# D*u added on TensorE: a diag(D) matmul under the transposes that bring the scan's output back

## What is computed

```python
xz = jnp.einsum('ble,de->bld', xn, W_in)
u, z = (xz[..., :DIN], xz[..., DIN:])
u = jax.nn.silu(conv(u))                     
dt, Bm, Cm = ...                              # from u
dA = jnp.exp(dt[..., None] * A)               # 16 states for each channel
dBu = dt[..., None] * Bm[:, :, None, :] * u[..., None]
h = dA * h + dBu ;  y = (h * C).sum(states)   # the scan over the 512 tokens
y = y + u * D
y = y * jax.nn.silu(z)
out = jnp.einsum('bld,ed->ble', y, W_out)
```

## Time and profile before

| | us |
|---|---|
| median of 3 runs | 1903.42 |
| lowest and highest run | 1899.98, 1903.66 |
| the profiled execution's time | 1908.13 |
| its span, first to last instruction | 1906.3 |

### The profile page before, as it was taken

How to read it: one execution, slowest core, us unless ns; L and a number is a source line. 1 busy time by engine, 2 the same in 40 slices (tenths; PEclk the granted TensorE clock), 3 DMA queues, 4 the chain that set the end, 5 groups by cost and what they waited for, 6 DMA issues and landing times. The chain is left out here.

```text
span 1906.3 us, 15651 instructions
## 1 busy us (share of the span) xinstructions
PE 1431.9 (75%) x5136; PEld 789.3 (41%) x5136; DVE 1516.7 (80%) x1606; ACT 937.5 (49%) x1481; POOL 793.6 (42%) x411
## 2 busy tenths in 40 slices
PE   5556676776788679976788679886788769876965
PEld 2345233343345235453355335453355334452433
DVE  3987699967898799969998699968999699963242
ACT  4432654435653655636553645626563555633522
POOL 0665165514554155523554156523555055530000
PEclk9555878786899879997899979997899979897987
DMA  5632342206221343205231343205231243200000
GB/s 179 234 122 78 123 143 101 88 24 211 94 105 45 124 143 111 89 24 199 100 109 54 101 146 119 99 22 190 99 110 66 74 160 132 99 11 0 11 1 22
DMA packets 64760, 188.86 MB, mean 99 GB/s; under 512 B 6224, under 2 KB 22480, under 8 KB 64720
## 3 DMA queue, kind: packets, MB, share of 16 engines
q1 hardware_dynamic: 64720, 188.37, 28.7%
HBM read 183.62 MB, written 4.72 MB: 99 GB/s over the span
## 5 line engine op out<-in xcount | busy, mean ns | idle before, releaser
L428 POOL TENSOR_TENSOR reg_a<-reg_a,cb 128x1024 f32<-128x1024 f32 x256 | 612.1, 2391 | 500.5 <-DVE reg_a L1070 499.5
L1070 DVE TENSOR_TENSOR_SCAN reg_a<-reg_a,pb 128x1024 f32<-128x1024 f32 x256 | 584.2, 2282 | 19.7 <-ACT reg_a L855 6.9
L624 PE MATMUL py<-ident,reg_a 128*128 128x128 f32 x2048 | 328.3, 317 | 101.5 <-POOL reg_a L428 101.5
L855 ACT ACTIVATE reg_a<-dt,neg_a 128x511 f32<-128x511 f32 x512 | 336.3, 710 | 101.4 <-DVE reg_a L1070 101.4
L624 PEld LDWEIGHTS py<-ident,reg_a 128*128 128x128 f32 x2048 | 278.3, 164 | 225.0 <-POOL reg_a L428 130.9
L1061 DVE TENSOR_TENSOR pb<-bb,pb 128x1024 f32<-128x1024 f32 x256 | 314.5, 1228 | 25.3 <-DVE reg_a L1070 0.5
L528 PE MATMUL px<-hT,whh 128*128 128x512 f32 x384 | 204.3, 658 | 0.0
L513 PE MATMUL px<-hT,gT 128*64 128x512 f32 x96 | 65.0, 815 | 100.9 <-ACT xs L743 100.9
L602 PE MATMUL pc<-x2T,w_fc 128*128 128x512 f32 x224 | 123.6, 680 | 20.1 <-DVE reg_y L1087 12.3
L761 ACT ACTIVATE xs<-px,half_b 128x512 f32<-128x512 f32 x96 | 66.1, 688 | 143.1 <-PE px L532 142.9
L532 PE MATMUL px<-an,vw 64*128 64x512 f32 x192 | 120.3, 709 | 16.2 <-DVE an L974 16.1
(11 more groups left out here) (162 smaller groups left out, 1975.9 us busy)
## 6 DMA issues: line engine op xcount, KB each, us to landing
bb<-bc_rows SPq DMA_DIRECT2D x256, 512.0 KB, 3.6
cb<-bc_rows SPq DMA_DIRECT2D x64, 512.0 KB, 5.9
xin<-x_in SPq DMA_DIRECT2D x9, 512.0 KB, 3.5
xs<-x_in SPq DMA_DIRECT2D x8, 512.0 KB, 3.5
x_out<-reg_m SPq DMA_DIRECT2D x8, 512.0 KB, 3.4
w_in<-w_inT_in SPq DMA_DIRECT2D x1, 1024.0 KB, 6.8
w_fc<-w_fcT_in SPq DMA_DIRECT2D x1, 1024.0 KB, 10.9
w_pr<-w_prT_in SPq DMA_DIRECT2D x1, 1024.0 KB, 13.1
```

What stands on the lines that cost most here:

```text
L428: pool.tensor_tensor(h[:, g % HR], h[:, g % HR], cb[:, 2 * q:2 * q + 2], ALU.mult).then_inc(s["hc_done"], 1)
L624: mm = pe.matmul(py[:, cols_], h[:, g % HR, j, cols_], ident[:], is_transpose=True, start=(q == 0 and j == 0 and i2 == 0), stop=(q == PAIR ...
L855: ins = act.activation(d_a[:, g % 2, j, 1:], dt[:, c, 1:], ACT.Exp, scale=neg_a[:, c * NS + n + j:c * NS + n + j + 1])
L1070: dve.tensor_tensor_scan(h2[:, g % HR], d_a2[:, g % 2], pb[:, 0:2, :].rearrange("p a t -> p (a t)"), 0.0, ALU.mult, ALU.add).then_inc(s["s ...
```

## The change

Four matrices diag(D/2) of 128x128 are made once, in the setup, on VectorE. `y_back` first multiplies u2 by diag(D/2) into the bank pc, and the four transposes then accumulate onto it. VectorE now multiplies the bank by the gate sz and writes yv; it tells so with `yz_done`. GpSimd's multiplication goes, and so does `ypost_done`.

```diff
@@ setup, tiles
         half_d = sb("half_d", [P, DT])
+        diag_d = sb("diag_d", [P, DT, P])
@@ GpSimd, scan loop
-                    if mamba and chunk_end(g) is not None:
-                        c = chunk_end(g)
-                        pool.wait_ge(s["ypost_done"], c + 1)
-                        pool.tensor_tensor(yv[:, c], yv[:, c], sz[:, c], ALU.mult).then_inc(s["yz_done"], 1)
@@ TensorE, unit_start
                 if back:
-                    pe.wait_ge(s["ypost_done"], back)
+                    pe.wait_ge(s["yz_done"], back)
@@ TensorE, y_back
                 pe.wait_ge(s["yt_ready"], c + 1)
+                pe.matmul(pc[:], diag_d[:, c], u2[:, c], start=True, stop=True)
                 for i2 in range(TT):
-                    mm = pe.transpose(pc[:, i2 * P:(i2 + 1) * P], yv[:, c, i2 * P:(i2 + 1) * P], ident[:])
+                    mm = pe.matmul(pc[:, i2 * P:(i2 + 1) * P], yv[:, c, i2 * P:(i2 + 1) * P], ident[:], is_transpose=True,
+                                   start=False, stop=True, skip_group_check=True)
                 mm.then_inc(s["yback_full"], 1)
@@ VectorE, setup
-            dve.tensor_scalar(half_d[:], cols[:, COLS["D"]], 0.5, None, ALU.mult)
+            dve.tensor_scalar(half_d[:], cols[:, COLS["D"]], 0.5, None, ALU.mult).then_inc(params_done, 1)
+            dve.wait_ge(params_done, 3)
+            for c in range(DT):
+                dve.tensor_scalar(diag_d[:, c], ident[:], half_d[:, c:c + 1], None, ALU.mult)
@@ VectorE, scan loop
                             dve.wait_ge(s["yback_full"], c + 1)
-                            dve.scalar_tensor_tensor(yv[:, c], u2[:, c], half_d[:, c:c + 1], pc[:], ALU.mult, ALU.add).then_inc(s["ypost_done"], 1)
+                            dve.tensor_tensor(yv[:, c], pc[:], sz[:, c], ALU.mult).then_inc(s["yz_done"], 1)
```

More of the change, by code:

```diff
@@ L85 @@
 z_full zth_ready sz_ready sp_abs sp_exp sp_ln dt_ready dtu_ready da_zero yt_ready yback_full
-bc_kept bc_out cb_in0 cb_in1 cb_in2 cb_in3 cb_in4 cb_in5 cb_in6 cb_in7 b_in0 b_in1 b_in2 da_ready mul_done scan_done hc_done hsum_done ypost_done yz_done
+bc_kept bc_out cb_in0 cb_in1 cb_in2 cb_in3 cb_in4 cb_in5 cb_in6 cb_in7 b_in0 b_in1 b_in2 da_ready mul_done scan_done hc_done hsum_done yz_done
 op_half op_full res_done post_stat post_aggr post_ve post_rs post_norm post_full hT_loaded
@@ L921, in _ @@
             dve.tensor_scalar(half_b[:], half_b[:], 0.5, None, ALU.mult)
-            dve.tensor_scalar(half_d[:], cols[:, COLS["D"]], 0.5, None, ALU.mult)
+            dve.tensor_scalar(half_d[:], cols[:, COLS["D"]], 0.5, None, ALU.mult).then_inc(params_done, 1)
+            dve.wait_ge(params_done, 3)
+            for c in range(DT):
+                dve.tensor_scalar(diag_d[:, c], ident[:], half_d[:, c:c + 1], None, ALU.mult)
             dve.tensor_scalar(g_scale[:], cols[:, COLS["slot_w"]], SCALE, None, ALU.mult)
             dve.tensor_scalar(w_x[:], w_x[:], 0.5, None, ALU.mult).then_inc(params_done, 1)
-            dve.wait_ge(params_done, 3)
+            dve.wait_ge(params_done, 4)
             dve.tensor_scalar(w_x[:, :, DTR:Q], w_x[:, :, DTR:Q], 0.5, None, ALU.mult)
```

## The result

The changed kernel is slower: 1922.18 us in the median of 5 runs, against 1903.42 before. Four of the five lie between 1917.44 and 1923.07; the fifth, 3589 us, is a disturbed execution, the profiled one, in which TensorE was busy for 3329.9 us. Over the four the ratio is 1.0082, 95% interval [1.0063, 1.0101], +15.6 us. A second series of the same kernel, run for this study as `e1_again`, gave 1919.58 us against 1906.95, ratio 1.0071 [1.0057, 1.0085], +13.5 us. Its profile (span 1917.8 us) is the one shown from here on as that of the changed kernel, beside the profile of before (span 1906.3), a pair that differs by 11.5 us, less than the medians do.

The account below looks back on a forecast made before the run. VectorE was taken to bound the scan loop and TensorE the stretch after it. Tail +6.9, third block +3.4 and VectorE -0.8 summed to +9.5 us, 1912.9 on the median, written as 1912.5, range 1902.5 to 1919.

Parts of the forecast that it names:

- What bounds the kernel: VectorE bounds the scan loop; after it TensorE runs without idle time from the last block's transposes and VectorE waits.
- GpSimd's product at nothing: Removing 32 GpSimd products (L432), 40 us in all, from loop and tail was costed at no gain.
- VectorE's instruction at -0.8: VectorE's new product is 0.07 us shorter, counting at 12 first and third blocks: -0.8 us, bounds 0 and -2.2.
- Setup: Four diag products and one more wait delay VectorE by less than 2 us, hidden behind TensorE's first projections.
- The tail: Fourth block: TensorE has no idle time from y_back on, so each added matmul costs 0.86 us, +6.9 us in eight.
- if the clock rises at the moment at which it rose before: Tail assumption: the matmul takes 1.71 us at the low level, but later records meet the high level sooner, leaving 0.86.
- Rival D: Tail's low stretch moves back with the work, or hsum's delayed transposes hold up more scans: +15, 1918 us; chance 0.12.
- the bound of 13.7 us: Tail's upper limit: if the clock's rise moves back with the work, each of eight matmuls costs 1.71 us.
- The third block: Slot 26: in four iterations TensorE has no idle time behind y_back, 0.86 us each, +3.4 us; bounds 0 and 6.0.
- B: Transposes don't count for the clock, the added matmul does; tail 3.4, first block also gains: +4, 1907.4 us; chance 0.21.
- C: The added matmul raises the clock at once, removing the low stretch heading the output projection: -3, 1900.4 us; chance 0.10.

Follow-up runs that it names:

- q2_no_gpsimd: Kernel before without GpSimd's product L432, the gate left out and yz_done signalled by VectorE: ratio 1.0008 against before, +1.5 us.
- q1_dve_only: Kernel before with VectorE's L1087 as a plain add of bank and u2, factor D left out: ratio 0.9998 against before, -0.4 us.
- q3_setup_only: Kernel before with the four diag(D) matrices made in the setup and used nowhere: ratio 1.0004 against before, +0.8 us.
- e5_no_fourth: Changed kernel with the diag(D) matmul in blocks 0 to 2 only, none in the tail: ratio 1.0027 against before, +5.1 us.
- v1_idle_slots: Changed kernel with all four diag(D) matmuls moved to where TensorE was idle and the bank free: 1886.46 us, ratio 0.9909 against before.
- r3_tail_slot33: Changed kernel with only the fourth block's matmul moved, to the head of slot 33: 1886.19 us, ratio 0.9910 against before.
- s1_before_idle_tr: Kernel before with eight unused 128x128 transposes per mamba iteration at the head of slot 33: ratio 0.9923 against before, -14.7 us.

## Why the prediction was wrong

The direction was right and the size too small: +9.5 us was forecast, +15.6 measured (+13.5 in the second series), and 1922.18 lies above the range's end of 1919. The profiled pair differs by 11.5 us, nearer to the sum, partly since the profiled execution of before was a long one (1908.13).

**What bounds the kernel: right.** The scan loops grew by 2.2 us in eight, the tails by 12.2.

**GpSimd's product at nothing: right.** q2_no_gpsimd is within its interval of before. In the changed kernel GpSimd's busy time fell by 47 us, where 40 were foreseen, and L429's waits for the scan grew by 21, not by as much as the busy time fell. At the fifth iteration's second block L977 (now L979) didn't get shorter, 1.68 us for 1.61 (in one iteration of seven it did, 1.22), as the reading of the earlier trace rows said. **VectorE's instruction at -0.8: right in kind.** It takes 0.69 us (0.67 to 0.68 was foreseen), and q1_dve_only shows no change that can be measured. **Setup: right.** The four products take 0.88 us together in the timeline, and q3_setup_only stands at 0.8 us with an interval of 2.7 either way:

```profile
11.83 0.88 DVE L924 TENSOR_SCALAR diag_d<-ident,half_d 128x128 f32<-128x128 f32 x4
```

**The tail: the term that was mis-sized.** It stood at 8 x 0.86 = 6.9 us and is 12.2, 1.52 each. The price of the matmul was right: 1.71 us at the low level were foreseen, 1.84 separate L630's and L632's starts in the eighth iteration (1702.85 and 1704.69). The step that failed is "if the clock rises at the moment at which it rose before", with the 0.86 us that it leaves. These are 8 us from the end of ScalarE's copy in the fourth tail, before and after, with a mean granted clock of 0.79 and 0.61, which makes 3.4 and 6.2 us at the low level:

```profile
823.56:831.56 8.00, 7.85 (x34) 6.85 (x35) 3.42 (x9) 0.00 (x1) 1.96 (x3) 0.79 0.00 0
829.21:837.21 8.00, 7.86 (x23) 5.79 (x24) 2.07 (x5) 0.00 (x0) 0.70 (x2) 0.61 0.01 2
```

Over the eight tails the granted clock was at the low level behind the copy for 3.7, 3.4, 4.3, 3.4, 4.2, 3.4, 0 and 2.9 us before, 25.3 in sum, and for 6.0, 5.5, 5.0, 6.3, 3.1, 3.2, 3.2 and 3.2 us in the changed kernel, 35.4 in sum. The term took the two sums to be equal. Records at the low level take twice the time, so half of the difference, 5.1 us, comes on top of the 6.9: 12.0 of the 12.2 measured, and tail by tail the same sum (0.86 plus half of what the low time grew) meets the measured one within 0.1 us. In the first four tails the rise came 0.7 to 2.8 us later, counted from the copy, than before; in the fifth, sixth and eighth it came from 1.1 us earlier to 0.3 later; and in the seventh a low stretch stands where there had been none (+2.4 us). Rival D named the later rise, as half of the way to the bound of 13.7 us, at a chance of 0.12. I had no ground to take the near end: the rows showed how long the low stretch lasted, not what its end was tied to. That stays open: the end neither kept its moment nor moved back by the work's length. Halfway between the two ends, 10.3 us, the sum would have been +12.9.

**The third block: +3.4 foreseen, not settled.** The third gap of L979 is 1.4 us in the last five iterations of the changed kernel, where before it was 1.07 to 1.41 in three; 1.9 was foreseen in those and 0 elsewhere. But where the gap is new, L979 is no longer stretched, and gap and length together grew by 0.34 to 0.36 us in the fourth to seventh iterations and didn't in the others: 1.4 us at this place, where the sum had 3.4. The line of the sixth iteration, answering to the earlier trace rows:

```profile
1248.98 1.23 DVE L979 SCALAR_TENSOR_TENSOR xs<-xs 128x1024 f32<-128x1024 f32 x1 [1.41 <-ACT xs L764]
```

The loops as a whole grew by 2.2 us, near the 3.4 - 0.8 of the sum, which is luck as far as this place goes. And e5_no_fourth, with the matmul in blocks 0 to 2 only, stands 6 us above its twin without, and moving these three out of the way (v1_idle_slots against r3_tail_slot33) gains nothing. What the three cost isn't settled by these runs.

**The rivals.** B rested on the premise that ordinary matmuls raise the clock and transposes don't. s1_before_idle_tr refutes the second half: eight transposes in the idle time gave -14.7 us, one matmul -12.8 us. They don't only keep the clock up, they also raise it. In the first tail of that kernel the clock had been at the low level since 103.8 us, with nothing but transposes on TensorE, and it rose at 178.9, behind 16 transposes in a row:

```profile
175.32 1.97 PE L624 MATMUL py<-ident,reg_a 128*128 128x128 f32 x8 [1.73 <-POOL reg_a L428]
177.08 1.92 PE L664 MATMUL pc<-ident,u 128*128 128x128 f32 x8
179.05 1.09 PE L624 MATMUL py<-ident,reg_a 128*128 128x128 f32 x8
```
```profile
175.50:178.80 3.30, 3.30 (x16) 3.09 (x15) 1.06 (x1) 0.00 (x0) 2.16 (x1) 0.50 0.31 97
178.90:182.00 3.10, 2.36 (x17) 1.95 (x17) 0.48 (x1) 0.60 (x1) 0.09 (x1) 1.00 0.17 59
```

The trace of the kernel before has such a place too: in the second iteration TensorE is idle for 8.96 us, runs 16 transposes from 386.80 to 390.37 (L554, L624) at the low level, and the granted clock is 1.00 from 390.1 to 393.6. So B's premise could have been refuted from the rows of before. The rule of the Trainium skill, TensorE: Matmul & The Clock Gate, section Part 4: PE-mode transpose, that transposes don't count as busy for the clock gate, doesn't hold for these f32 transposes, with which the granted clock was 1.00 from 1671 to 1674 and from 1676 to 1682; the measurement decides. C, that the tail begins at the high level, is the mechanism of the kernels that are faster, only that it takes the matmul ahead of the idle time's end, not behind it. D was the nearest to what happened, with 10.3 us for the tail.

## What to carry to other kernels

Work that is put behind a wait of the engine that bounds a stretch moves everything behind it, and after idle time it runs at the slow pace: here a matmul of 0.86 us at the high level cost 0.4 to 2.4 us a tail. When its inputs are ready, put it ahead of the wait, into the idle time. Before costing an added instruction in such a place, look at how long the engine was idle just before, at what level its clock stands behind that, and for how long: here the same change was worth +13.5 us with one matmul in one place and -17.1 with it in the other. And where single runs of one kernel spread over 10 us, a second series is worth more than a narrow interval of the first: a gain of 8.2 us was 0.8 in the second, on another chip.

## What the hardware showed unexpectedly

- Useless work makes the kernel faster. One unused matmul per iteration in TensorE's idle time before the tail gave -12.8 us (interval 9.1 to 16.4), eight unused transposes -14.7 us (11.2 to 17.9); with the transposes the granted clock was 1.00 in the eighth tail from 1676 to 1682, where the kernel before had 0.50 at the head of its tail.
- Transposes in f32 (128x128, 0.11 us each at the high level) count for the clock as a f32 matmul in the same place does: none of the eight tails had a low stretch with either, and in the first the clock rose to 1.00 behind 16 transposes in a row, with no other work on TensorE before them in the scan loop.
- Added time that is no work of TensorE's can cost more than itself: 8.4 us of ScalarE copies made the kernel 12.8 us slower (8.8 to 16.6).
